# First 16-head attention: one exponential per head straight from the score bank, and the turned queries and keys copied by VectorE

## The reference, cut to what matters

```python
q = (emb @ Wq.T).reshape(B, SQ, N_HEADS, KQ_DIM).transpose(0, 2, 1, 3)
k = (context @ Wk.T).reshape(B, SK, N_HEADS, KQ_DIM).transpose(0, 2, 1, 3)
v = (context @ Wv.T).reshape(B, SK, N_HEADS, KQ_DIM).transpose(0, 2, 1, 3)
q = _layernorm(q, qn_w, qn_b)
k = _layernorm(k, kn_w, kn_b)
attn = jnp.einsum('bhqd,bhkd->bhqk', q, k) * scale
attn = jax.nn.softmax(attn, axis=-1)
out = jnp.einsum('bhqk,bhkd->bhqd', attn, v)
out = out.transpose(0, 2, 1, 3).reshape(B, SQ, N_HEADS * KQ_DIM)
return out @ Wu.T + bu
```

## Time and profile before

| | |
|---|---|
| median of three runs | 1511.34 us |
| the profiled execution | 1512.01 us, span 1510.2 us |
| busy in the span: PE, DVE, ACT, POOL | 1288.7, 876.2, 703.4, 277.0 us |
| the stage in the span | 168 to 454 us |

### The profile page before, as it was taken

One profiled execution on the slowest core, in us unless ns is written; L12 is line 12 of the kernel. 1 busy time (PEld: TensorE's weight loads), 2 busy tenths in 40 slices (PEclk: granted clock), 3 DMA queues, 4 the chain that ended last, 5 costly groups with the idle time before them and its releaser, 6 DMA issues. The chain is left out here.

```text
span 1510.2 us, 26211 instructions
## 1 busy us (share of the span) xinstructions
PE 1288.7 (85%) x8587; PEld 959.7 (64%) x8587; DVE 876.2 (58%) x2280; ACT 703.4 (47%) x1529; POOL 277.0 (18%) x382
## 2 busy tenths in 40 slices
PE   6767589989987899599999978972999987999995
PEld 5742356666664577477777758861677763676664
DVE  4539788888864454556666544448687752122225
ACT  4323487777763112245555542531455533333343
POOL 1010032222221000023323230022434420000000
PEclk9869699999997999799999999975899978999998
DMA  9000000000000000000000005020000000000000
GB/s 346 1 1 0 1 1 2 1 1 2 1 1 1 1 1 1 0 2 1 2 2 1 2 13 114 2 110 2 1 1 0 0 1 0 1 1 1 0 1 29
DMA packets 6426, 24.48 MB, mean 16 GB/s; under 512 B 797, under 2 KB 1311, under 8 KB 5418
## 3 DMA queue, kind: packets, MB, share of 16 engines
q1 hardware_dynamic: 6314, 23.03, 4.5%
HBM read 21.98 MB, written 1.05 MB: 15 GB/s over the span
## 5 line engine op out<-in xcount | busy, mean ns | idle before, releaser
L1305 DVE SCALAR_TENSOR_TENSOR XN<-bank,gate,XN 128x128 f32<-128x128 f32 x256 | 89.8, 351 | 224.7 <-PE bank L1269 222.2
L1285 ACT ACTIVATE e_hidden<-bank,small 128x512 f32<-128x512 f32 x152 | 104.4, 687 | 214.5 <-PE bank L1257 214.5
L745 POOL TENSOR_TENSOR a_pn<-a_probs,a_rec 128x512 f32<-128x512 f32 x128 | 133.0, 1039 | 365.7 <-DVE a_rec L995 241.3
L1269 PEld LDWEIGHTS bank<-attention_weights,e_hidden 128*128 128x128 f32 x1024 | 119.2, 192 | 14.8 <-issue 14.8
L1009 DVE TENSOR_REDUCE a_mx<-bank 128x4 f32<-128x512 f32 x128 | 86.8, 678 | 65.4 <-PE bank L807 65.4
L1257 PE MATMUL bank<-XNT,attention_weights 128*128 128x512 f32 x256 | 121.3, 607 | 1.2 <-PEq L541 1.2
L1269 PE MATMUL bank<-attention_weights,e_hidden 128*128 128x128 f32 x1024 | 119.4, 275 | 0.0
L1017 DVE TENSOR_TENSOR a_shifted<-bank,a_mx 128x512 f32<-128x512 f32 x128 | 88.3, 690 | 3.5
L990 DVE TENSOR_REDUCE a_total<-a_probs 128x4 f32<-128x512 f32 x128 | 86.6, 677 | 3.6 <-ACT a_probs L947 3.5
L1900 PEld LDWEIGHTS bank<-blk_va,blk_pT 128*128 128x128 f32 x512 | 64.3, 193 | 33.7 <-issue 22.4
L833 PE MATMUL bank<-attention_weights,a_cv 128*128 128x512 f32 x128 | 72.6, 649 | 14.9 <-issue 14.8
(11 more groups left out here) (351 smaller groups left out, 2613.3 us busy)
## 6 DMA issues: line engine op xcount, KB each, us to landing
attention_weights<-in_a SPq DMA_DIRECT2D x2, 2048.0 KB, 11.0
mod_ring<-in_mod_weights SPq DMA_DIRECT2D x4, 576.0 KB
ctx_both<-in_ctx SPq DMA_DIRECT2D x1, 2048.0 KB, 9.8
attention_weights<-in_up SPq DMA_DIRECT2D x1, 2048.0 KB, 7.8
attention_weights<-in_down SPq DMA_DIRECT2D x1, 2048.0 KB, 12.3
down<-in_down SPq DMA_DIRECT2D x1, 1536.0 KB, 17.3
down<-in_mod_weights SPq DMA_DIRECT2D x2, 576.0 KB
X<-in_x SPq DMA_DIRECT2D x4, 256.0 KB, 3.7
```

Source lines behind the costliest of these rows:

```text
L745: pool.tensor_tensor(pn[:, p, :].rearrange("p (h s) -> p h s", h=4), probs[:, p, :].rearrange("p (h s) -> p h s", h=4), rec[:, p, :].unsqu ...
L1269: last = pe.matmul(down_bank[j][:, 0:width], layer[0:rows, f, j * 128:(j + 1) * 128], down(g, f), start=f == 0, stop=f == NB - 1)
L1285: act.activation(hidden[0:rows, p, f, :], up_bank_of(i, f)[0:rows, :], function, bias=up_bias(g, f)).then_inc(hidden_ready, 1)
L1305: dve.scalar_tensor_tensor(out=total, in0=down_bank[j][:, e * D:(e + 1) * D], scalar=gate_column(k, 4 * q + j, g * per_group + e), in1=tot ...
```

## The change

With `qk_norm` given, three things change. ACT no longer takes one exponential of 128 x 512 from `shifted`: `head_exponentials` takes four of 128 x 128, one for each head, straight from the score bank, with minus the scaled maximum as bias, and each also leaves its sum in `total`. DVE no longer subtracts nor adds up; a small step `lower` scales the maxima. And the copy of turned queries and keys moves from ACT to DVE (`keep_normed_qk`), ahead of everything else in DVE's turn. The exponentials move from lag 7 to lag 6, behind the logarithm and exponential of the norm in ACT's turn, and the scores of a pair now wait for `exped` in place of `subtracted`.

```diff
-        lag = {..., "subtract": 6, "exponentials": 7,
+        lag = {..., "subtract": 6, "exponentials": 6,
...
-                    await_count(pe, subtracted, m)
+                    await_count(pe, exped if qk_norm is not None else subtracted, m)
...
+            def head_exponentials(i):
+                m, p = i.number, i.slot(2)
+                await_count(act, lowered, m + 1)
+                if i.older_than(2):
+                    await_count(act, p_normed, m - 1)
+                for h in range(4):
+                    last = act.activation(probs[:, p, h * S:(h + 1) * S], score_bank[p][:, h * S:(h + 1) * S], ACT.Exp,
+                                          bias=low[:, p, h:h + 1], scale=W ** -0.5, accum_out=total[:, p, h:h + 1])
+                last.then_inc(exped, 1)
...
+            def lower(i):
+                m, p = i.number, i.slot(2)
+                await_count(dve, maxed, m + 1)
+                if i.older_than(2):
+                    await_count(dve, exped, m - 1)
+                dve.tensor_scalar(low[:, p, :], mx[:, p, :], -W ** -0.5, None, ALU.mult).then_inc(lowered, 1)
+
+            def keep_normed_qk(i):
+                m, (b, g), p = i.number, i.part(4), (i.offset // 4) % 2
+                await_count(dve, qk_turned, m + 1)
+                if g == 0 and i.older_than(8):
+                    await_count(dve, scored, 4 * b - 4)
+                c = 0 if g < 2 else 2
+                dve.tensor_scalar((qT if g < 2 else kT)[:, p, (g % 2) * 512:(g % 2) * 512 + 512], qkt_bank[:, :],
+                                  qk_norm[:, c:c + 1], qk_norm[:, c + 1:c + 2], ALU.mult, ALU.add).then_inc(qk_kept, 1)
```

More of the change, by code:

```diff
@@ L693, in stage_head_attention @@
     if qk_norm is not None:
-        lag = {"square": 1, "turn_qk": 2, "keep_qk": 3, "scores": 6, "project_v": 6, "subtract": 6, "exponentials": 7,
+        lag = {"square": 1, "turn_qk": 2, "keep_qk": 3, "scores": 6, "project_v": 6, "subtract": 6, "exponentials": 6,
                "sums": 7, "turn_p": 9, "keep_p": 9, "values": 11, "keep_o": 11, "out": 12, "normalise": 13, "turn_x": 13}
@@ L709, in stage_head_attention @@
             sq, ssq, qn = sb("sq", [128, 512]), sb("ssq", [128, 2, 8]), sb("qn", [128, 2, 512])
+            low = sb("low", [128, 2, 4])
         staged, v_staged = sem("staged"), sem("v_staged")
@@ L716, in stage_head_attention @@
         v_projected, v_kept, weighted = sem("v_projected"), sem("v_kept"), sem("weighted")
-        totalled, inverted, p_normed, o_kept = sem("totalled"), sem("inverted"), sem("p_normed"), sem("o_kept")
+        lowered, totalled, inverted, p_normed, o_kept = sem("lowered"), sem("totalled"), sem("inverted"), sem("p_normed"), sem("o_kept")
         y_done, bias_spread, biased = sem("y_done"), sem("bias_spread"), sem("biased")
@@ L907, in keep_qk @@
                 m, (b, g), p = i.number, i.part(4), (i.offset // 4) % 2
-                await_count(act, qk_turned if qk_norm is not None else qk_projected, m + 1)
-                bank = qkt_bank if qk_norm is not None else project_bank[i.slot(projects)]
+                await_count(act, qk_projected, m + 1)
                 if g == 0 and i.older_than(8):
                     await_count(act, scored, 4 * b - 4)
[L912 to L919, removed]
+                act.activation((qT if g < 2 else kT)[:, p, (g % 2) * 512:(g % 2) * 512 + 512],
+                               project_bank[i.slot(projects)][:, :], ACT.Copy).then_inc(qk_kept, 1)
             def rstd_qk(i):
@@ L953, in body @@
                     square(at(lag["square"]))
-                if at(lag["exponentials"]).alive:
+                if qk_norm is None and at(lag["exponentials"]).alive:
                     exponentials(at(lag["exponentials"]))
-                if at(lag["keep_qk"]).alive:
+                if qk_norm is None and at(lag["keep_qk"]).alive:
                     keep_qk(at(lag["keep_qk"]))
@@ L961, in body @@
                     rstd_qk(at(lag["square"]))
+                if qk_norm is not None and at(lag["exponentials"]).alive:
+                    head_exponentials(at(lag["exponentials"]))
                 if at(lag["keep_o"]).alive and at(lag["keep_o"]).offset % 2 == 1:
@@ L989, in total_up @@
                 await_count(dve, exped, m + 1)
-                dve.tensor_reduce(total[:, p, :], probs[:, p, :].rearrange("p (h s) -> p h s", h=4), AX.X,
-                                  ALU.add).then_inc(totalled, 1)
-                await_count(dve, totalled, m + 1)
+                if qk_norm is None:
+                    dve.tensor_reduce(total[:, p, :], probs[:, p, :].rearrange("p (h s) -> p h s", h=4), AX.X,
+                                      ALU.add).then_inc(totalled, 1)
+                    await_count(dve, totalled, m + 1)
                 if i.older_than(2):
@@ L1022, in body @@
             def body(at):
+                if qk_norm is not None and at(lag["keep_qk"]).alive:
+                    keep_normed_qk(at(lag["keep_qk"]))
                 if qk_norm is not None and at(lag["square"]).alive:
@@ L1026, in body @@
                     maxima(at(lag["scores"]))
+                    if qk_norm is not None:
+                        lower(at(lag["scores"]))
                 if at(lag["normalise"]).ends_batch:
                     norm.normalise(dve, batch_of(at(lag["normalise"])))
-                if at(lag["subtract"]).alive:
+                if qk_norm is None and at(lag["subtract"]).alive:
                     subtract(at(lag["subtract"]))
```

## The result

The changed kernel takes 1571.7 us (median of 4 runs, 1570.9 to 1573.2) against 1511.5 us (4 runs, 1510.7 to 1512.3) for the kernel before in the same comparison: ratio 1.0399, 95% interval 1.0381 to 1.0417, 60 us slower. 1552 was forecast, in a range of 1530 to 1585. The profiled execution took 1571.66 us, span 1569.8.

What follows compares the result with a forecast made beforehand. DVE, waiting only for ACT's square, was taken as the bound before; then one chain through each turn adds 28.7 us steady, 8.3 first turns, 1 fill, 2 drain: 40 on 1512.0, said as 1552 us, range 1530 to 1585.

Steps and rivals of the forecast that it cites:

- Cases A and B: Rivals: A faster, DVE's work per item 0.45 us shorter, 1488 us (chance 0.05); B no difference, ACT has slack, 1511 (0.03).
- DVE's ring is the bound: Kernel before, steady batch: DVE's 14.32 us busy plus 2.3 waiting for the square make 16.6 of 17.06 us.
- The chain's terms: Each turn, square through sums, maxima and exponentials to next square: 4.02 us odd, 4.98 even, plus 0.45 a pair.
- The head's price: On ACT, one head's exponential with its sum read-out takes 0.345 us between starts, 1.38 us an item.
- cases C and D: Rivals: C read-out doesn't overlap, 0.57 a head, 1604 us (0.07); D it hides and 0.45 us delay doesn't arise, 1518 (0.09).
- The step 0.45 us late: On DVE, sums of squares start 1.08 us after the square instead of 0.63, behind the new copy, once a pair.
- case E: Rival: PE gets a lower clock for part of the stage, 10 to 30 us more, 1562 to 1582 (chance 0.10).
- The scores wait, but it is covered by 0.5 us: A pair's scores wait for the previous turn's exponentials; maxima are due 1.72 us after these, scores in 1.2: no cost.
- The count of batches: Steady part, square 14 to 64: 12.6 batches at 2.28 us more each, 28.7 us.
- The first turns: Square 6 to 14, without output and norm steps yet: eight turns take 35.0 us against 26.65, 8.3 more.
- The fill: Start of the stage: the new copy ahead of the sums of squares costs 0 to 2 us, taken 1.
- The drain: End of the stage: five exponentials remain without squares, chained behind their maxima, 1 to 3 us more, taken 2.

Runs made afterwards that it cites:

- e10: Changed kernel with maxima and scaled maxima first on DVE, exponentials right behind the square on ACT, and their sum back on DVE without read-outs: 1546.1 us.
- e9: Kernel before with only the copy of turned queries and keys moved to DVE, first in its turn: 1525.5 us.
- e3: Changed kernel with the copy of turned keys and queries back on ACT, behind the square: 1538.8 us.
- e5b: Changed kernel with 8 spare 128x128 matmuls on PE ahead of the scores of each batch's first pair: 1557.1 us.
- e4: Changed kernel with the sum of the exponentials back on DVE, so no read-outs on ACT: 1544.4 us.
- e12: e2 with DVE's reciprocal moved from the end of its turn to just behind the scaled maxima, so POOL's product starts later: 1515.4 us.
- e5: Changed kernel with 16 spare 128x128 matmuls on PE ahead of the scores of each batch's first pair: 1577.0 us.
- e2: The better order: changed kernel with DVE taking maxima, scaled maxima, copy, then sums of squares, and ACT the exponentials directly behind the square: 1520.4 us.

## Why the prediction was right, and where it was off

- **What decides is order, not load: right, and shown for this set of instructions.** The same instructions in another order take 1520 us. Cases A and B (faster or no change because DVE is relieved) rested on the load and fell. Neither half of the new order helps alone, as one chain through both engines would have it. Order isn't all, though: with the sum back on DVE the better order gains nothing (e10).
- **"DVE's ring is the bound": wrong, without harm to the sum.** It added DVE's busy time to its waits, but the durations overlap by 0.07 to 0.09 us each, 29 times in the batch. A copy more per item on DVE (e9) lengthened the batch by 0.61 us and not by 2.9.
- **The chain's terms: right.** The batch's turns from 333.45 on take 4.95, 4.57, 5.97 and 4.99 us; forecast were 4.98, 4.47, 4.98 and 4.47 + 0.44. Three of four are within 0.1. The head's price, 0.345, was right, and with it cases C and D fell. One sign was named the wrong way round: the prediction's last paragraph has the sums of squares wait for the square on odd turns and for the copy on the others, and the trace (as its own working) has the copy's delay on the odd turns.
- **The copy's size: off by 0.07 to 0.15.** It was taken at 0.65 between starts, from neighbours in the earlier trace rows. It lasts 0.81 and the next instruction starts 0.73 behind it. The step 0.45 us late became 0.56: (339.60 - 338.40) is 1.20 from square to sums in place of 0.63, and where the copy doesn't stand in the way it is 0.65. That is the likely part of the 0.15 us by which the three other turns of a batch exceed the forecast, 1.9 us from square 14 on.
- **The clock: left out of the sum.** "In the steady part it had 1.00" was the argument against case E, and it looked at a PE that never stood still for 2 us. Case E happened on top of the forecast, not in place of it: 13 turns between square 14 and 64 take 1.0 us longer, 12.8 us, and with spare work in the gap the same stretch is 12.3 us shorter (244.4 us in place of 256.7). "The scores wait, but it is covered by 0.5 us" was true at full clock and blind to what the wait does to the clock: with scores of 2.06 us the maxima wait 0.47. By the prediction's own signs (a clock under 1.00 in the steady part) this part of it was wrong. The measured 1571.7 lies in case E's 1562 to 1582, which had a chance of 0.10, and inside the range because the range took in E.
- **The count of batches: 1.5 us too many.** Square 14 to 64 are 50 turns, 12 batches and two turns. By the prediction's own terms they take 12 x 19.34 + 4.98 + 4.91 = 242.0 us, 27.2 more than before, where 12.6 x 2.28 gave 28.7.
- **The first turns: mis-sized.** The turns from square 6 to 14 take 4.82, 4.57, 4.87, 4.74, 4.51, 4.56, 5.93 and 4.54 us. Three were put at 4.0, without copies of values and without the delay; both are there from the first item on. That is 2.3 us, and the slow clock 0.9 in the seventh.
- **The fill: about right.** The table's 2.3 starts from a first square that came early: before, PE's first four projections took 3.78 us, now 1.98. From ACT's last copy ahead of the stage to the sixth square it is 14.95 us before (from 166.94) and 16.21 now (from 165.34), 1.3 more where 1 was taken. The new copy is what costs it: with the copy back on ACT (e3) the same piece takes 14.50 us.
- **The drain: too small.** 5.8 us more, where 2 was taken. With spare work (e5b) it takes 35.85 us in place of 37.42, at a clock of 1.00 in place of 0.94; without read-outs (e4) 34.41, also at 1.00. So about 1.6 us are the clock and 1.4 the read-outs. The other 2.8 no experiment separates; the copy alone (e9) has a drain 2.2 us longer than the kernel before. The better order has no longer a drain that costs so much (34.8 us in e12).

So the direction and the main mechanism were right. Of the 19 us between the forecast for the stage (40) and its 59.3, about 15 are the clock (12.8 in the steady part, 0.9 in the first turns, 1.6 in the drain), 2 the other turns of a batch, 2.3 the miscounted first turns and 2.2 the rest of the drain. Against them stand 1.5 us of batches counted too many and 1.6 us by which the stages ahead ran shorter in this trace. Why no order found here beats the kernel before stays partly open: the steady batch can (16.88 us), the ends of the stage don't.

## What to carry to other kernels

Moving work off the busiest engine helps only if the order on the others lets it start early: before counting load, write down for one turn what stands ahead of each moved step on its new engine, and follow the chain to the next turn. When a change gives PE a new wait, don't only ask whether the wait is covered; look at the granted clock behind waits of that length elsewhere in the trace. And try a new order on both engines at once: each half alone was worse here (14 and 37 us) where the pair gained 51.

## What the runs showed of the hardware

- **A slow clock behind a gap.** PE was idle for 2.14 us ahead of the scores and then worked 4.3 us at a granted 0.60, most of it at the lower of the two levels (1.2 in place of 2.4 GHz). Behind gaps of 1.63 and 1.78 us, in the kernels with copy or sum moved back, the clock stayed at 1.00. The gap alone doesn't settle it. In the changed kernel scores took 1.16 us behind gaps of 2.35 and 2.19 us too, the first of them with slow matmuls right behind it (1.77 us for a projection that takes 1.10), as the rows below show. And in the drain of the kernel with the copy back on ACT (e3) scores took 2.08 us behind a wait of only 0.71.

```profile
191.20 1.16 PE L808 MATMUL bank<-a_kT,a_qT 64*128 64x128 f32 x16 [2.35 <-ACT a_probs L949]
...
192.29 1.77 PE L834 MATMUL bank<-attention_weights,a_cv 128*128 128x512 f32 x2
...
200.34 1.16 PE L808 MATMUL bank<-a_kT,a_qT 64*128 64x128 f32 x16 [2.19 <-ACT a_probs L949]
```

- **Spare matmuls bought time**: 8 a batch, some 1.95 us of PE each time, took 14.6 us off (e5b); 16 a batch, 3.74 us, added 5 (e5).
- **A step of 128x4 can be held up by POOL**: a median of 0.34 us and up to 0.54 beside POOL's 1.04 us product (e2), a median of 0.17 with POOL started later (e12).
- **A copy from a bank with two scalars per partition** takes 0.81 us for 128x512, a plain one 0.67. The reading out of a sum takes 0.2 us as an instruction, and 0.09 between starts (341.38 to 341.47).
